# A transformer block on one core: the written-out order of steps, attention of sequence 0 ahead of sequence 1

## The reference, cut to what matters

```python
sa, ca, ga, sb, cb, gb = silu(c) @ wmod                  # per sequence; ga, gb are clipped in size
h = layernorm(x) * (1 + ca) + sa
x = x + ga * attn_block(h)                               # below
h = layernorm(x) * (1 + cb) + sb
x = x + gb * moe(h)                                      # 16 experts of 176, top 4, and a shared one of 352

def attn_block(x):                                       # 16 heads of 16
    h = layernorm(x); x_conv = silu(causal_conv4(h))
    q, k = l2norm(h @ Wq), l2norm(h @ Wk); v = layernorm_per_head(h @ Wv)
    u = sigmoid(x_conv @ Wig) * k * v; gamma = sigmoid(x_conv @ Wg)
    mem[t] = gamma[t] * mem[t-1] + u[t]                  # a linear recurrence in place of attention
    out = groupnorm(layernorm(mem) * q) * sigmoid(x_conv @ Wog)
    h = x + out @ Wo
    return h + (silu(h2 @ Wgate) * (h2 @ Wval)) @ Wout   # h2 = layernorm(h), 1024 wide
```

## Time and profile before

| | us |
|---|---|
| median of 3 runs | 424.5 (424.0 to 424.7) |
| the profiled execution | 423.7, of which the profile's span is 421.9 |
| PE busy | 382.1 (91%) |
| DVE busy | 271.4 (64%) |
| ACT busy | 199.0 (47%) |
| POOL busy | 114.6 (27%) |
| chain that ended last | PE 66%, DVE 19%, ACT 9%, issue 3% |

### The profile page before, as it was taken

The page is one execution under the profiler, slowest core; times in us unless marked ns, Lnnn a source line. Parts: engine busy times, 40 slices in busy tenths (PEclk is TensorE's granted clock), DMA queues, the critical chain, the costliest instruction groups (busy, mean ns, idle before and its releaser), DMA issues.

```text
span 421.9 us, 4540 instructions
## 1 busy us (share of the span) xinstructions
PE 382.1 (91%) x1588; PEld 290.4 (69%) x1588; DVE 271.4 (64%) x429; ACT 199.0 (47%) x310; POOL 114.6 (27%) x96
## 2 busy tenths in 40 slices
PE   3769796977699999999989999999999999999993
PEld 1548563524268878887777888888888888888872
DVE  3897996758666446575888555555556555655763
ACT  1526628996583253374465333433343334344331
POOL 1344595002423000113433311221122112224310
PEclk9959898999699999999999999999999999999998
DMA  8700021001320000002543263224432543124321
GB/s 277 268 0 2 0 63 38 0 2 34 114 99 28 1 2 0 0 15 90 153 142 115 60 198 124 87 87 145 118 88 92 146 113 89 42 93 132 120 76 50
DMA packets 18646, 34.80 MB, mean 82 GB/s; under 512 B 2464, under 2 KB 5920, under 8 KB 18624
## 3 DMA queue, kind: packets, MB, share of 16 engines
q1 hardware_dynamic: 18624, 34.52, 26.1%
HBM read 33.39 MB, written 1.11 MB: 82 GB/s over the span
## 4 chain that ended last, share of the span: by engine, by line
PE 66%; DVE 19%; ACT 9%; issue 3%; DMA 1%; SPq 0%; DVEq 0%; ACTq 0%
PE ps L1219 10%; PE ps L1220 10%; PE ps L1221 10%; PE ps L1247 5%; PE ps L1244 5%; PE ps L1243 5%; DVE w L763 4%; PE ps L1170 3%; PE ps L1175 3%; PE ps L1171 3%; PE ps L1003 2%; PE ps L1020 2%; PE ps L1004 2%; ACT w L433 2%; ACT w L434 2%
## 5 line engine op out<-in xcount | busy, mean ns | idle before, releaser
L345 POOL TENSOR_TENSOR wsm_lo<-w,wsm_hi 128x768 fp32r<-128x768 f32 (+1 forms) x40 | 71.4, 1785 | 182.5 <-ACT wsm_hi L618 170.3
L1219 PE MATMUL ps<-b_hi,wsm_hi 128*128 128x512 f32 x200 | 79.5, 398 | 0.0
L1220 PE MATMUL ps<-b_hi,wsm_lo 128*128 128x512 f32 x200 | 79.1, 395 | 0.0
L1221 PE MATMUL ps<-b_lo,wsm_hi 128*128 128x512 f32 x200 | 79.1, 395 | 0.0
L630 ACT ACTIVATE a_hi<-w 128x512 fp32r<-128x512 f32 x50 | 31.6, 632 | 92.3 <-DVE w L957 92.2
L953 DVE TENSOR_TENSOR w<-w,gate_b 128x512 f32<-128x512 f32 x44 | 47.4, 1077 | 39.5 <-ACT w L624 39.4
L962 DVE TENSOR_TENSOR a_lo<-w,a_hi 128x512 fp32r<-128x512 f32 x50 | 34.6, 692 | 32.8 <-ACT a_hi L630 32.8
L624 ACT ACTIVATE w<-ps 128x512 f32<-128x512 f32 x50 | 29.7, 595 | 31.5 <-PE ps L1221 31.5
L1219 PEld LDWEIGHTS ps<-b_hi,wsm_hi 128*128 128x128 f32 x200 | 37.6, 188 | 9.5 <-DVE w L957 0.5
L1221 PEld LDWEIGHTS ps<-b_lo,wsm_hi 128*128 128x128 f32 x200 | 37.6, 188 | 9.1
L1220 PEld LDWEIGHTS ps<-b_hi,wsm_lo 128*128 128x128 f32 x200 | 37.6, 188 | 8.8
(11 more groups left out here) (147 smaller groups left out, 625.1 us busy)
## 6 DMA issues: line engine op xcount, KB each, us to landing
w<-in_wmoe SPq DMA_DIRECT2D x33, 384.0 KB, 3.2
gate_b<-w_rows SPq DMA_DIRECT2D x16, 256.0 KB, 4.3
w<-in_x SPq DMA_DIRECT2D x4, 512.0 KB, 4.5
stage<-in_wff SPq DMA_DIRECT2D x4, 512.0 KB, 6.8
gate_b<-w_rows SPq DMA_DIRECT2D x8, 224.0 KB, 3.5
w<-in_wmod SPq DMA_DIRECT2D x3, 512.0 KB, 6.3
w<-in_wsm SPq DMA_DIRECT2D x3, 512.0 KB, 8.3
gate_b<-w_rows SPq DMA_DIRECT2D x8, 192.0 KB, 3.5
```

The source lines that it names most:

```text
L345: return nc.gpsimd.tensor_tensor(lo, raw, f32(hi), ALU.subtract)
L1219: mm(bank, mgu(wsm_hi, slot, k, which), b_hi[b][:, k, :], start=k == 0, stop=False)
L1220: mm(bank, mgu(wsm_lo, slot, k, which), b_hi[b][:, k, :], start=False, stop=False)
L1221: last = mm(bank, mgu(wsm_hi, slot, k, which), b_lo[b][:, k, :], start=False, stop=k == KC - 1)
```

## The change

The four strings are replaced. Each holds the same steps as before, once each, and no operation, buffer or wait is added or taken out. Each sequence's own steps keep their order except for independent ones; what moves is how the two sequences, the splits of weights and the steps of the experts are interleaved.

```diff
--- before.py
+++ after.py
@@ -76,42 +76,41 @@
 
 
 TENSOR_PLAN = """
-    shift.0 shift.1 modulation.0 modulation.1 t1.0 q.0 t1.1 k.0 q.1 k.1 v.0 ig.0 ga.0 ssk.0 og.0 v.1 ssv.0 ig.1
-    ga.1 u.0 ssk.1 mem.0 og.1 oc.0 vo.0 ssv.1 wo.0 tw.0 u.1 mem.1 oc.1 t2.0 vo.1 up.0.0 wo.1 up.0.1 tw.1
-    down.0.0 up.0.2 down.0.1 up.0.3 down.0.2 up.0.4 down.0.3 t2.1 up.0.5 down.0.4 up.0.6 down.0.5 up.0.7
-    down.0.6 down.0.7 up.1.0 tm.0 up.1.1 down.1.0 up.1.2 down.1.1 up.1.3 down.1.2 up.1.4 t3.0 down.1.3 up.1.5
-    logits.0 down.1.4 up.1.6 down.1.5 up.1.7 wt.0 down.1.6 down.1.7 tm.1 eup.0.0 eup.0.1 edown.0.0 eup.0.2
-    edown.0.1 eup.0.3 edown.0.2 t3.1 eup.0.4 edown.0.3 eup.0.5 logits.1 edown.0.4 eup.0.6 edown.0.5 wt.1 eup.0.7
-    edown.0.6
+    shift.0 shift.1 modulation.0 modulation.1 t1.0 q.0 k.0 v.0 t1.1 ig.0 q.1 ssk.0 ga.0 v.1 k.1 og.0 ig.1 ga.1 ssv.0
+    ssk.1 og.1 u.0 mem.0 ssv.1 oc.0 vo.0 u.1 wo.0 tw.0 mem.1 oc.1 t2.0 vo.1 up.0.0 up.0.1 wo.1 up.0.2 tw.1 down.0.0
+    up.0.3 up.0.4 down.0.1 down.0.2 up.0.5 t2.1 down.0.3 down.0.4 up.0.6 up.0.7 down.0.5 down.0.6 down.0.7 up.1.0 tm.0
+    up.1.1 up.1.2 down.1.0 up.1.3 t3.0 down.1.1 up.1.4 down.1.2 logits.0 up.1.5 up.1.6 wt.0 down.1.3 eup.0.0 down.1.4
+    up.1.7 eup.0.1 eup.0.2 edown.0.0 down.1.5 down.1.6 down.1.7 eup.0.3 tm.1 edown.0.1 eup.0.4 edown.0.2 eup.0.5 t3.1
+    edown.0.3 edown.0.4 logits.1 eup.0.6 edown.0.5 eup.0.7 wt.1 edown.0.6
 """
 
 SCALAR_PLAN = """
-    shift.0 shift.1 wsm.0 wsm.1 gate.0 wsm.2 chunk.0 chunk.1 gate.1 h1.0 q.0 h1.1 wsm.3 wsm.4 wsm.5 wsm.6 k.0
-    xconv.0 v.0 q.1 k.1 ig.0 ga.0 xconv.1 og.0 rk.0 v.1 rv.0 ig.1 ga.1 sqm.0 rm.0 og.1 sqo.0 ro.0 rk.1 gated.0
-    rv.1 wo.0 chunk.2 sqm.1 rm.1 chunk.3 sqo.1 chunk.4 h2.0 ro.1 gated.1 silu.0.0 chunk.5 wo.1 hid.0.0 silu.0.1
-    hid.0.1 silu.0.2 hid.0.2 silu.0.3 hid.0.3 silu.0.4 hid.0.4 silu.0.5 hid.0.5 h2.1 silu.0.6 hid.0.6 silu.0.7
-    hid.0.7 acc.0 silu.1.0 hid.1.0 silu.1.1 hid.1.1 silu.1.2 hid.1.2 silu.1.3 hid.1.3 silu.1.4 hid.1.4 h3.0
-    silu.1.5 hid.1.5 exp.0 ehigh.0.0 silu.1.6 hid.1.6 silu.1.7 ehigh.0.1 hid.1.7 acc.1 ehigh.0.2 esilu.0.0
-    ehid.0.0 ehigh.0.3 esilu.0.1 ehid.0.1 ehigh.0.4 esilu.0.2 ehid.0.2 ehigh.0.5 esilu.0.3 ehid.0.3 ehigh.0.6
-    esilu.0.4 h3.1 ehid.0.4 ehigh.0.7 esilu.0.5 exp.1 ehid.0.5 ehigh.0.8 esilu.0.6 ehid.0.6 ehigh.0.9 esilu.0.7
-    ehid.0.7
+    shift.0 wsm.0 gate.0 wsm.1 shift.1 gate.1 h1.0 q.0 wsm.2 wsm.3 xconv.0 k.0 h1.1 wsm.4 v.0 ig.0 q.1 chunk.0 rk.0
+    wsm.5 wsm.6 ga.0 k.1 xconv.1 og.0 v.1 chunk.1 ig.1 ga.1 rv.0 rk.1 chunk.2 og.1 sqm.0 rm.0 rv.1 sqo.0 ro.0 gated.0
+    chunk.3 wo.0 sqm.1 rm.1 sqo.1 h2.0 ro.1 silu.0.0 gated.1 hid.0.0 silu.0.1 hid.0.1 chunk.4 wo.1 silu.0.2 ehigh.0.0
+    chunk.5 hid.0.2 silu.0.3 ehigh.0.1 silu.0.4 ehigh.0.2 hid.0.3 silu.0.5 hid.0.4 ehigh.0.3 h2.1 hid.0.5 silu.0.6
+    hid.0.6 silu.0.7 hid.0.7 acc.0 silu.1.0 hid.1.0 silu.1.1 hid.1.1 silu.1.2 hid.1.2 silu.1.3 h3.0 hid.1.3 silu.1.4
+    hid.1.4 exp.0 silu.1.5 hid.1.5 silu.1.6 esilu.0.0 hid.1.6 ehid.0.0 esilu.0.1 silu.1.7 ehid.0.1 esilu.0.2 ehigh.0.4
+    hid.1.7 ehid.0.2 acc.1 esilu.0.3 ehid.0.3 ehigh.0.5 esilu.0.4 ehid.0.4 esilu.0.5 ehigh.0.6 h3.1 ehigh.0.7 ehid.0.5
+    exp.1 esilu.0.6 ehigh.0.8 ehid.0.6 esilu.0.7 ehid.0.7 ehigh.0.9
 """
 
 VECTOR_PLAN = """
-    var0.0 var0.1 scaled0.0 shifted.0 var1.0 scaled0.1 shifted.1 var1.1 hn1.0 vsum scaled modc hn1.1 h1lo.0
-    modg.0 modg.1 h1lo.1 conv.0.0 conv.0.1 xlo.0 conv.1.0 conv.1.1 a1.0 xlo.1 gamma.0 uk.0 uv.0 mem.0 a1.1
-    gamma.1 o1.0 osig.0 gated.0 uk.1 outlo.0 uv.1 wo.0 mem.1 var2.0 o1.1 osig.1 hn2.0 h2lo.0 gated.1 outlo.1
-    prod.0.0 hidlo.0.0 prod.0.1 wo.1 var2.1 hidlo.0.1 prod.0.2 hidlo.0.2 prod.0.3 hidlo.0.3 hn2.1 prod.0.4
-    hidlo.0.4 prod.0.5 hidlo.0.5 prod.0.6 hidlo.0.6 prod.0.7 hidlo.0.7 h2lo.1 prod.1.0 hidlo.1.0 sum3.0 gated3.0
-    prod.1.1 plus_x.0 hidlo.1.1 var3.0 prod.1.2 hidlo.1.2 prod.1.3 hn3.0 hidlo.1.3 prod.1.4 hidlo.1.4 h3lo.0
-    prod.1.5 lgsub.0 hidlo.1.5 topk.0 prod.1.6 hidlo.1.6 prod.1.7 hidlo.1.7 wt.0 sum3.1 gated3.1 egated.0.0
-    plus_x.1 elo.0.0 var3.1 egated.0.1 elo.0.1 egated.0.2 elo.0.2 hn3.1 egated.0.3 elo.0.3 egated.0.4 h3lo.1
-    elo.0.4 egated.0.5 lgsub.1 topk.1 elo.0.5 egated.0.6 elo.0.6 egated.0.7 elo.0.7 wt.1
+    var0.0 scaled0.0 shifted.0 var1.0 modc scaled var0.1 hn1.0 scaled0.1 shifted.1 h1lo.0 conv.0.0 vsum var1.1 conv.0.1
+    hn1.1 xlo.0 h1lo.1 conv.1.0 conv.1.1 a1.0 xlo.1 uk.0 a1.1 uv.0 gamma.0 mem.0 uk.1 o1.0 osig.0 uv.1 gamma.1 gated.0
+    outlo.0 mem.1 wo.0 var2.0 o1.1 hn2.0 osig.1 h2lo.0 gated.1 prod.0.0 outlo.1 hidlo.0.0 modg.0 prod.0.1 hidlo.0.1
+    prod.0.2 wo.1 var2.1 hidlo.0.2 prod.0.3 hidlo.0.3 prod.0.4 hn2.1 prod.0.5 hidlo.0.4 hidlo.0.5 prod.0.6 modg.1
+    prod.0.7 hidlo.0.6 h2lo.1 hidlo.0.7 prod.1.0 sum3.0 gated3.0 hidlo.1.0 prod.1.1 plus_x.0 var3.0 hidlo.1.1 prod.1.2
+    hn3.0 hidlo.1.2 prod.1.3 prod.1.4 hidlo.1.3 lgsub.0 topk.0 prod.1.5 h3lo.0 hidlo.1.4 wt.0 hidlo.1.5 egated.0.0
+    prod.1.6 elo.0.0 hidlo.1.6 egated.0.1 prod.1.7 egated.0.2 hidlo.1.7 elo.0.1 elo.0.2 egated.0.3 sum3.1 gated3.1
+    plus_x.1 var3.1 egated.0.4 hn3.1 elo.0.3 elo.0.4 egated.0.5 lgsub.1 elo.0.5 topk.1 egated.0.6 elo.0.6 egated.0.7
+    h3lo.1 elo.0.7 wt.1
 """
 
 POOL_PLAN = """
-    rstd.0.0 rstd.1.0 wsm.0 rstd.0.1 rstd.1.1 wsm.1 vcentre wsm.2 wsm.3 wsm.4 sqk.0 wsm.5 sqv.0 wsm.6 sqk.1
-    chunk.0 chunk.1 sqq.0 sqq.1 sqv.1 chunk.2 rstd.0.2 chunk.3 chunk.4 chunk.5 rstd.1.2 rstd.0.3 elow.0 elow.1 elow.2 elow.3 rstd.1.3 elow.4 elow.5 elow.6 elow.7
+    rstd.0.0 rstd.0.1 wsm.0 rstd.1.0 wsm.1 wsm.2 vcentre wsm.3 rstd.1.1 sqk.0 wsm.4 chunk.0 wsm.5 wsm.6 sqk.1 sqq.0
+    sqv.0 chunk.1 chunk.2 sqv.1 chunk.3 sqq.1 rstd.0.2 chunk.4 elow.0 chunk.5 elow.1 elow.2 rstd.1.2 elow.3 rstd.0.3
+    elow.4 elow.5 rstd.1.3 elow.6 elow.7
 """
 
 
```

## The result

| | before | after |
|---|---|---|
| median of the runs beside each other | 424.6 us | 412.4 us (4 runs, 411.5 to 413.4) |
| ratio after to before | | 0.9701, 95% interval 0.9682 to 0.9721 |
| the profiled execution, and its span | 423.7, 421.9 us | 411.5, 409.7 us |

The kernel is faster by 12.7 us (0.0299 x 424.6). The forecast was 7.2 us of gain, 417.3 us, and a range that began at 412.0; by the ratio the time is 411.9 us. The profiled execution is the fastest of its four. Where an experiment is compared with the kernel after, 0.9697 stands for both: 411.7 us.

A forecast was written before the change was run, and what follows sets the result against it. Bound: an attention chain passing between VectorE, ScalarE and TensorE, ahead of TensorE's dense work. Lead 6.9 + 0.8 = 7.7, less 0.5 for a low clock, gives 7.2 us: 417.3 us by the median, range 412 to 423.

The forecast's parts named there:

- low clock at a further place: TensorE at the lower clock at one more place, taken off the lead at the loop: 0.5 us.
- Part 1: Head, to 45 us: hn1.0 1.4 us later, yet conv.0.0 at 30.4 in place of 37.23; h1.1 at 44.9.
- Part 2: ScalarE's list, 45 to 79 us: 34.2 us of unbroken steps, sqm.0 at 79.1, only 0.3 us gained.
- Part 3: End of attention, 79 to 111 us: sequence 1's done work pays; up.0.0 at 110.7, 7.5 us ahead.
- Part 4: Wide layer, 111 to 125 us: up.0.1 waits 1 us, down.0.0 at 124.6, lead 6.9 us.
- Part 5: 125 to 227 us, to the loop: pairs of up fit, fewer waits; +0.8 us, bounds -3 to +1.
- (a): Clock stays up at both places, head starts early: 2 to 3 us better, 414.5 us; chance 0.2.
- (b): Wide layer: eight close pairs of up stall 0.7 to 1 us each, 423.9 us, no change; chance 0.08.
- (c): TensorE stays at 1.2 GHz from mem.0 to up.0.0: 11 us, 428; decides from 7 us; chance 0.07.
- (d): Two or three late inputs in ScalarE's unbroken list, half the gain: 420.5 us; chance 0.2.

The follow-up runs named there:

- experiment 8: The kernel after, unaltered, measured once more on the chip of three other runs: ratio 0.9693, 411.6 us.
- Experiment 1: Kernel after with GpSimd's list beginning rstd.0.0 rstd.1.0 wsm.0 rstd.0.1, as the prediction took it to be: ratio 0.9816, 416.8 us.
- experiment 4: Kernel before with sequence 0's normalisation first on VectorE and GpSimd: 427.2 us; plus modg moved later: 427.8; plus its convolution ahead of sequence 1's steps: 421.4.
- experiment 5: Kernel after with wsm.2 and wsm.3 earlier on ScalarE and vsum earlier on VectorE: ratio 0.9694, 411.6 us.
- experiment 2: Kernel after's attention order, kernel before's order behind: 416.5 us, 412.4 with modg and chunk.4 placed elsewhere; the reverse combination: 423.8 us.
- e9_after_again: The run of experiment 8, the kernel after unaltered: ratio 0.9693, 411.6 us; its profiled execution took 413.2 us.

## Why the prediction was wrong, and where it was right

The direction and the way the new order helps were right, the size was not: 7.2 us forecast, 12.7 measured. The account goes by the distances between the prediction's marks in the two profiled executions, one of each kernel; by experiment 8 single rows of it are good to 1 or 2 us.

| stretch | predicted | measured | gives |
|---|---|---|---|
| start to `h1.0` | 26.9 | 22.90 | +4.0 |
| `h1.0` to `conv.0.0` | 3.5 | 4.2 | -0.7 |
| `conv.0.0` to `v.0` | 9.4 | 9.3 | +0.1 |
| `v.0` to `h1.1` | 5.1 | 5.55 | -0.4 |
| `h1.1` to `sqm.0` | 34.2 | 34.7 | -0.5 |
| `sqm.0` to `hn2.0` | 24.5 | 24.6 | -0.1 |
| `hn2.0` to `up.0.0` | 7.1 | 5.45 | +1.6 |
| `up.0.0` to `down.0.0` | 13.9 | 13.9 | 0 |
| lead gained from there to the loop | 0.8 | 1.4 | +0.6 |
| low clock at a further place | 0.5 | 0 | +0.5 |

The sum is 5.1, and 12.2 (the two spans) less 7.2 is 5.0. In the second row `h1lo.0` starts only at 25.89, behind `shifted.1` of sequence 1 (24.30, 1.67 us), though its first input was there at 24.35.

**The step that failed is the first one of Part 1**, "`var0.1`, which `rstd.0.1` waits for". In these names the sequence stands before the last number of `rstd`, and the norm behind it: `rstd.0.1` is the second norm of sequence 0 and waits for `var1.0`, which in `var` is written the other way round. The section on the kernel before had it right (`rstd.b.1`), the prediction read it wrongly and placed `hn1.0` 1.4 us later than before, where it starts 2.3 us earlier. In the profiled execution of after the loads came 0.8 us late (`var1.0`'s start and `shift.0`, 11.61 against 10.81), so that on equal loads the step is 4.8 us wrong. So the wait that the prediction put ahead of `hn1.0` isn't there. Experiment 1 shows it: in the order as misread, `hn1.0` starts at 23.11 (23.4 was predicted), behind a wait of 4.03 us for its `rstd`, and the time is 416.8 us (417.3 was), 5.1 above the kernel after. That the total then agrees so closely also needed the forecast's other errors to cancel.

**Part 1, the rest.** `v.0` behind `wsm.2`, `vcentre` and `wsm.3` was right: 9.3 us behind the convolution, with a wait of 3.38 (3.4 was predicted). That `modg` and `hn1.1` ahead of `conv.0.0` were what the old order lost was only partly so: experiment 4 shows that in the old order `modg` lay in a wait for sequence 1's `h1.1`, and was free; moving sequence 1's steps was not.

**Part 2** held to half a us over 34 us, although its reason was incomplete: a list summed by durations gives the right length when its engine is full, but experiment 5 shows that TensorE would hold the place if ScalarE did not.

**Part 3** was right in its order of events, and 1.6 us off by the clock: it priced `oc.1` and `t2.0` at 1.2 GHz. Experiment 8 shows that both happen: from `hn2.0` to `up.0.0` it has 7.5 us, where 7.1 were predicted and 5.45 measured in the kernel after. So this 1.6 us is the luck of one execution and no error of the order; a price should have been given for both levels of the clock.

**Part 4** was right to 0.1 us, the wait of `up.0.1` included (1.12, predicted 1). **Part 5**: its +0.8 was +1.4 in the traces, and 0.7 to 0.8 by the two halves of experiment 2, neither clear of nothing.

**The clock.** Behind `v.0`'s wait of 3.38 us half of its matmuls ran slow, as was assumed; at `mem.0` the granted clock from 77.3 to 84 us was 0.75. The price of a product at the lower clock, "twice that" (5.6 us), was a little high: within `v.0` a matmul starts 0.43 us behind the one before it from 37.53 on, against 0.233 at the higher clock, which is 5.1 us for 12.

**The rivals.** (a) More gain by an earlier head and the clock at full speed: this is where the time went, though not for the reason given; the bound of 2 to 3 us for it was too narrow, since it took no account of a misread wait. (b) Stalls in the close pairs of `up`: refuted by the lead that grows from 10.9 us at `down.0.0` (8.1, and the 2.8 of the `up` done by then) to 12.3 at the loop, and by the two halves. (c) A low clock through the sparse stretch: the windows from 90 to 105 us stayed at 1.00 in the profile of after. In that of `e9_after_again` the clock fell to 0.50 from 99.9 to 105.5 us, so the mechanism is there, at a cost near 2 us and not 7 to 11. (d) Late inputs in ScalarE's list: the largest from `h1.1` to `sqm.0` is 0.62 us.

## What to carry to other kernels

When a prediction walks lists written by hand, the first wait must be checked against the function that makes it (which semaphore, which index), not against the step's name: here one exchanged index cost 4 to 5 us, and what stood behind it was right to 0.7 us in each stretch, the clock aside. On an engine that is kept in order, look first for steps that wait for the second item's data ahead of the first item's critical step (here worth 6.4 us, experiment 4); whether a step between them costs anything depends on whether a wait already covers it, and only a run that moves it tells. Before a split or a copy is moved later, follow what its end releases on the queue that issues the loads, down to the last load behind it. And before two profiles are compared at a late mark, compare them at an early one that the edit can't reach.
